# Four graph-attention layers on one core: the target scores of layers 0 and 2 go through DRAM instead of through TensorE

## The reference, cut to what matters

```python
# layer 0
f1 = (h @ W.T) @ a1;  f2 = (h @ W.T) @ a2            # a score per node: source, target
e = leaky_relu(f1[:, None] + f2[None, :], 0.2)
attn = softmax(where(adj == 0, -1e9, e), axis=-1)
x = x + elu(attn @ h)       # h >= 0 and attn >= 0, so elu changes nothing
# layer 2
e = leaky_relu((h @ w_src)[:, None] + (h @ w_dst)[None, :] + b, 0.2)
attn = softmax(where(adj + eye == 0, -inf, e), axis=-1)
x = x + attn @ h
```

## Time and profile before

| | |
|---|---|
| runs | 3770.13, 3774.3, 3774.59 us, median 3774.3 |
| profiled execution | 3771.3 us, of which the span of the trace is 3769.4 |
| TensorE busy | 3567.6 us, 95% of the span |
| VectorE busy | 3088.7 us, 82% |
| ScalarE, GpSimd busy | 52% and 50% |
| mean granted TensorE clock | 0.986 of full speed |

### The profile page before, as it was taken

The page is one execution under the profiler, slowest core; times in us unless marked ns, Lnnn a source line. Parts: engine busy times, 40 slices in busy tenths (PEclk is TensorE's granted clock), DMA queues, the critical chain, the costliest instruction groups (busy, mean ns, idle before and its releaser), DMA issues.

```text
span 3769.4 us, 75317 instructions
## 1 busy us (share of the span) xinstructions
PE 3567.6 (95%) x25488; PEld 3231.1 (86%) x25488; DVE 3088.7 (82%) x6892; ACT 1949.1 (52%) x4770; POOL 1867.9 (50%) x2852
## 2 busy tenths in 40 slices
PE   3899999999999999999999999999999999999996
PEld 2788888888888888888888888888888888888885
DVE  6788888888888888888888888888888888888874
ACT  2455555555555555555555555555555555555552
POOL 4355455445455545555554554554555545545543
PEclk7999999999999999999999999999999999999997
DMA  3000000000000000000000000000000000000000
GB/s 122 14 20 20 26 20 20 26 20 20 23 23 20 20 26 20 20 26 20 20 26 20 20 26 20 20 26 20 20 26 20 20 26 20 20 23 23 20 16 12
DMA packets 62512, 90.10 MB, mean 24 GB/s; under 512 B 9265, under 2 KB 25777, under 8 KB 62129
## 3 DMA queue, kind: packets, MB, share of 16 engines
q1 hardware_dynamic: 62128, 85.30, 6.9%
HBM read 51.72 MB, written 33.55 MB: 23 GB/s over the span
## 4 chain that ended last, share of the span: by engine, by line
PE 73%; DVE 16%; ACT 5%; issue 4%; POOL 1%; DVEq 0%; ACTq 0%; POOLq 0%
PE bank_c L360 20%; PE bank_b L360 18%; PE bank_e L360 10%; PE bank_e L401 6%; DVE product L805 5%; PE bank_a L368 4%; PE bank_e L380 4%; PE bank_e L335 3%; PE bank_b L335 3%; DVE g L1045 2%; DVE x L831 2%; DVE nlE L1016 2%; DVE nlE L1028 2%; ACT g_hi L740 2%; ACT xa L702 2%
## 5 line engine op out<-in xcount | busy, mean ns | idle before, releaser
L598 ACT ACTIVATE h<-x,rs 128x512 f32<-128x512 f32 x384 | 311.8, 812 | 383.5 <-POOL rs L1114 383.5
L360 PE MATMUL bank_c<-w_hi,g_hi 128*128 128x258 f32 x2048 | 433.2, 293 | 76.4 <-ACT g_hi L740 75.7
L1109 POOL TENSOR_SCALAR rs<-mv 128x1 f32<-128x1 f32 x512 | 142.0, 277 | 688.3 <-DVE mv L798 659.4
L1189 POOL TENSOR_TENSOR nlE<-nlE,nmE 128x512 f32<-128x512 f32 x256 | 265.9, 1038 | 416.1 <-DVE nmE L1036 416.1
L360 PE MATMUL bank_c<-w_lo,g_hi 128*128 128x258 f32 x2048 | 413.3, 283 | 0.0
L360 PE MATMUL bank_b<-w_lo,hT_hi 128*128 128x344 f32 x1536 | 409.3, 321 | 0.0
L360 PE MATMUL bank_b<-w_hi,hT_hi 128*128 128x344 f32 x1536 | 408.7, 320 | 0.0
L360 PEld LDWEIGHTS bank_c<-w_hi,g_hi 128*128 128x128 f32 x2048 | 314.8, 189 | 97.4 <-ACT g_hi L740 96.4
L360 PE MATMUL bank_c<-w_hi,g_lo 128*128 128x258 f32 x2048 | 350.7, 283 | 0.0
L360 PE MATMUL bank_b<-w_hi,hT_lo 128*128 128x344 f32 x1536 | 345.8, 320 | 0.0
L656 ACT ACTIVATE hT_hi<-bank_e 128x512 fp32r<-128x512 f32 x128 | 76.7, 600 | 499.6 <-PE bank_e L352 499.6
(11 more groups left out here) (158 smaller groups left out, 10294.7 us busy)
## 6 DMA issues: line engine op xcount, KB each, us to landing
x_in<-in_x SPq DMA_DIRECT2D x128, 256.0 KB, 2.6
out<-out_sb SPq DMA_DIRECT2D x128, 256.0 KB, 2.0
adj_in<-in_adj SPq DMA_DIRECT2D x128, 64.0 KB, 2.5
pTE<-in_L_gnn_att_src SPq DMA_DIRECT2D x1, 512.0 KB, 4.2
pE<-in_L_gnn_att_dst SPq DMA_DIRECT2D x1, 512.0 KB, 5.1
xl<-in_L_gnn_W SPq DMA_DIRECT2D x1, 512.0 KB, 6.0
x<-in_L_gnn_W SPq DMA_DIRECT2D x2, 256.0 KB, 5.7
out_sb<-in_L_gnn_W SPq DMA_DIRECT2D x2, 256.0 KB, 6.4
```

Source lines behind the costliest of these rows:

```text
L360: last = mm(bank[:, 0:width], a[:, c * P:(c + 1) * P], w[:, c, b * width:(b + 1) * width], start=(first and c == chunks[0] and n == 0), st ...
L598: activation(h[layer][:, 0, :], src, ACT.Relu, bias=rs[layer][:, 2:3], scale=rs[layer][:, 1:2])\
L1189: tt(nlE[:, half, :], nlE[:, half, :], nm, ALU.subtract).then_inc(sem(f"L3_shifted{i}"), 1)
```

## The change

TensorE no longer makes scores for layers 0 and 2: `scores_L0` and `scores_L2` are gone, and the waits that guarded `bank_a` move to the transposes of the exponentials. SP writes the target column to a small DRAM tensor, waits until it is there, and reads it back as a row in all 128 partitions (`t_all`), in a new step `spread_targets`. VectorE adds row, source column and mask in one instruction from SBUF. The target rows are negated once at the start, and the bias of layer 2 becomes the start value of the source column's sum. In SP's turn the new steps stand after the weight chunks: layer 2's, then the store, then layer 0's.

```diff
+        t_all = {i: sb(f"t_all{i}", [P, P]) for i in (0, 2)}
+        t_dram = {i: nc.dram_tensor(f"t_dram{i}", [2, P], F32, kind="Internal").ap() for i in (0, 2)}
...
+            def spread_targets(layer, g):
+                key, s = f"L{layer}", g.slot(2)
+                sp.wait_ge(sem(f"st_made{layer}"), g.made())
+                sp.wait_ge(sem(f"t_spread{layer}"), 16 * g.made(1))
+                sp.dma_start(t_dram[layer][s].rearrange("(n a) -> n a", a=1), st[layer][:, 1:2])\
+                    .then_inc(sem(f"t_sent{layer}"), 16)
+                sp.wait_ge(sem(f"t_sent{layer}"), 16 * g.made())
+                sp.wait_ge(sem(f"{key}_v"), g.made(1))
+                sp.dma_start(t_all[layer][:], t_dram[layer][s:s + 1, :].to_broadcast([P, P]))\
+                    .then_inc(sem(f"t_spread{layer}"), 16)
...
             def turn(t):
                 if t.graph(0).live:
                     load(t.graph(0))
-                if t.graph(6).live:
-                    store(t.graph(6))
                 if t.loop is None and t.step == 0:
                     load_rest()
                 if t.loop is None and t.step in (1, 2, 3):
                     stage_weights(prepared[t.step])
+                if t.graph(4).live:
+                    spread_targets(2, t.graph(4))
+                if t.graph(6).live:
+                    store(t.graph(6))
+                if t.graph(0).live:
+                    spread_targets(0, t.graph(0))
...
-                def scores_L0():
...
-                        masks_and_t(bank_a, m_l, m_r, [st[0][:, 1:2]]).then_inc(sem("L0_scores"), 1)
...
                 def turn_exp_L0():
                     if A.live:
                         pe.wait_ge(sem("L0_exp"), A.made())
+                        pe.wait_ge(sem("x1_made"), A.made(1))
+                        pe.wait_ge(sem("x3_made"), A.made(4))
...
-                def scores_L2():
...
-                        masks_and_t(bank_a, m_l, m_r, [st[2][:, 1:2]]).then_inc(sem("L2_scores"), 1)
...
                 def turn_exp_L2():
                     if Dg.live:
                         pe.wait_ge(sem("L2_exp"), Dg.made())
+                        if A.live:
+                            pe.wait_ge(sem("x1_made"), A.made())
+                        else:
+                            pe.wait_ge(sem("x3_made"), Dg.made(1))
...
+            first_of = {0: 0.0, 2: attn_b_all[:]}
+
-            def score_columns(layer, g, scores):
+            def score_columns(layer, g):
 
                 dve.wait_ge(sem(f"h_made{layer}"), g.made())
-                dve.wait_ge(sem(scores), g.made(1))
-                for i, row in enumerate((s_row, t_row)):
-                    last = nc.vector.tensor_tensor_reduce(product[:, layer + i, :], h[layer][:, 0, :], row[layer][:], 1.0, 0.0,
+                dve.wait_ge(sem(f"t_sent{layer}"), 16 * g.made(1))
+                dve.wait_ge(sem(f"L{layer}_v"), g.made(1))
+                for i, (row, first) in enumerate(((s_row, first_of[layer]), (t_row, 0.0))):
+                    last = nc.vector.tensor_tensor_reduce(product[:, layer + i, :], h[layer][:, 0, :], row[layer][:], 1.0, first,
                                                           ALU.mult, ALU.add, st[layer][:, i:i + 1])
...
+            def softmax_spread(layer, g, m):
+
+                key = f"L{layer}"
+                dve.wait_ge(sem(f"t_spread{layer}"), 16 * g.made())
+                dve.wait_ge(sem("masks_made"), g.made())
+                dve.wait_ge(sem(f"{key}_exp"), g.made(1))
+                stt(nl1[key][:], t_all[layer][:], st[layer][:, 0:1], m, ALU.add, ALU.add)\
+                    .then_inc(sem(f"{key}_v"), 1)
+                least(key, g)
...
-                        nc.vector.tensor_copy(t_row[0][:], bank_e[:, 1, :]).then_inc(sem("rows_made"), 1)
+                        ts(t_row[0][:], bank_e[:, 1, :], -1.0, None, ALU.mult).then_inc(sem("rows_made"), 1)
...
-                        ts(s_row[2][:], s_row[2][:], -1.0, None, ALU.mult).then_inc(sem("rows_made"), 1)
-                        dve.wait_ge(sem("rows_made"), 5)
+                        for row in (s_row[2], t_row[2], attn_b_all):
+                            ts(row[:], row[:], -1.0, None, ALU.mult).then_inc(sem("rows_made"), 1)
+                        dve.wait_ge(sem("rows_made"), 7)
...
-                        softmax_one("L0", A, bank_a[:, 0:P], st[0][:, 0:1])
+                        softmax_spread(0, A, mask[:, A.slot(MR), :])
...
-                        softmax_one("L2", Dg, bank_a[:, 0:P], st[2][:, 0:1], attn_b_all[:])
+                        softmax_spread(2, Dg, mask_loop[:, Dg.slot(MR), :])
```

More of the change, by code:

```diff
@@ L561, in turn @@
                 turn_h1()
-                scores_L0()
                 project_L1b_first()
@@ L569, in turn @@
                 scores_L1a()
-                scores_L2()
                 turn_h3()
@@ L798, in stats, with softmax_one, least @@
                 nc.vector.bn_aggr(mv[layer][:], bn[layer][:]).then_inc(sem(f"mv_made{layer}"), 1)
-            def score_columns(layer, g, scores):
+            first_of = {0: 0.0, 2: attn_b_all[:]}
+            def score_columns(layer, g):
                 dve.wait_ge(sem(f"h_made{layer}"), g.made())
-                dve.wait_ge(sem(scores), g.made(1))
-                for i, row in enumerate((s_row, t_row)):
-                    last = nc.vector.tensor_tensor_reduce(product[:, layer + i, :], h[layer][:, 0, :], row[layer][:], 1.0, 0.0,
+                dve.wait_ge(sem(f"t_sent{layer}"), 16 * g.made(1))
+                dve.wait_ge(sem(f"L{layer}_v"), g.made(1))
+                for i, (row, first) in enumerate(((s_row, first_of[layer]), (t_row, 0.0))):
+                    last = nc.vector.tensor_tensor_reduce(product[:, layer + i, :], h[layer][:, 0, :], row[layer][:], 1.0, first,
                                                           ALU.mult, ALU.add, st[layer][:, i:i + 1])
                 last.then_inc(sem(f"st_made{layer}"), 1)
-            def softmax_one(key, g, bank, ns, bias=None):
+            def softmax_one(key, g, bank, ns):
                 dve.wait_ge(sem(f"{key}_scores"), g.made())
                 dve.wait_ge(sem(f"{key}_exp"), g.made(1))
[L813 to L816, removed]
+                ts(nl1[key][:], bank, ns, None, ALU.add).then_inc(sem(f"{key}_v"), 1)
+                least(key, g)
[6 more added lines that the diff above has]
+                    .then_inc(sem(f"{key}_v"), 1)
+                least(key, g)
+            def least(key, g):
                 dve.wait_ge(sem(f"{key}_v"), g.made())
@@ L900, in columns_L2 @@
                     if Dg.live:
-                        score_columns(2, Dg, "L2_scores")
+                        score_columns(2, Dg)
                 def hT_lo_L1a():
@@ L920, in columns_L0 @@
                     if N0.live:
-                        score_columns(0, N0, "L0_scores")
+                        score_columns(0, N0)
                 def values_L1a():
```

## The result

| | before | after |
|---|---|---|
| runs on the same chip, median | 3773.91 us | 4642.37 us (4639.17 to 4645.38) |
| ratio, 95% interval | | 1.2304 [1.2282, 1.2325] |
| span of the profiled execution | 3769.4 us | 4637.3 us |
| mean granted TensorE clock | 0.986 | 0.915 |

The change makes the kernel 23% slower. I had forecast 3777 us with a range up to 3805: wrong by 865 us, in size and in kind.

What follows compares the result with a forecast made beforehand. TensorE sets the pace for 20.4 us of the 28.37 us turn, VectorE for 8.0. Turns give -0.06 us x 122 = -7.3 us, start-up +11.3, together +4.0; forecast 3777 us, range 3758 to 3805.

Steps and rivals of the forecast that it cites:

- the way over DRAM in the steady state: First-layer target column to DRAM and back as a row: 5.3 us against 7.2 us available, 1.9 us of cover.
- The rule named beside the sum: For the DRAM transfers: the skill's some 2.0 us fixed per transfer, so about 4 us for both.
- the row comes late: Rival: two transfers need over 7.2 us, stalling VectorE at the first-layer addition; 0.9 us x 122 = 110 us, 3885; chance 0.13.
- Start-up: Once, SP's new waits delay the `w2` chunk, turn 2's row and `w3` chunks: plus 11.3 us, bounds 6 and 13.
- Loads behind the row: SP's queue: next loads issued ten microseconds later, landing at about 2041, before their use after 2042.24; costs nothing.
- the hole: TensorE idle after the first layer's score matmuls, awaiting `g_hi`: widens from 0.62 to about 0.95 us, gain 0.00 us.
- The transposes of `turn_h3`: TensorE, third layer: start 0.15 us after VectorE's result, take 0.63 instead of 0.60 us; gain 0.13 us a turn.
- The first-layer addition: VectorE, both inputs now in SBUF: 0.35 instead of 0.34 us, plus 0.01 us a turn.
- the port rival: GpSimd's one-element step holds VectorE's first-layer addition: +0.08 to +0.29 us a turn, 3787 to 3812 us; chance 0.17.
- The start value: VectorE's products of `columns_L2`: per-partition `attn_b_all` instead of 0.0 costs 0.06 us a turn, bounds 0.00 and 0.06.
- The third-layer addition: VectorE: 0.05 us shorter but held beside GpSimd's output addition, ending at 2028.25 against 2028.26; worth nothing.
- The whole 0.33 us comes back: Rival: `out_read` doesn't bind TensorE at the third layer; 0.20 x 122 = 24 us more gain, 3753 us; chance 0.05.

Runs made afterwards that it cites:

- the fastest transfers: Changed kernel with the first layer's column written 512 bytes apart, the third's to SBUF, rows read from constants (other ends of the transfers): 3776.32 us.
- the line in both layers: Changed kernel with each column gathered into one SBUF partition's line, sent to DRAM in one 512-byte piece, then to all partitions: 3783.39 us, ratio 1.0026.
- the first experiment: Changed kernel with first- and third-layer additions taking the target row of the graph before, so none waits for a fresh row: 3826.43 us, ratio 1.0139.
- the run without a reader: Changed kernel with columns written at 8 bytes (first layer) and 4 bytes (third) from element to element, neither read back, rows constant: 3866.78 us.

## Why the prediction was wrong

**The step that failed** is the way over DRAM in the steady state, in the words of the prediction: "2.0 + 0.6 for the write, 0.1 to wake SP, 2.6 for the row: 5.3 us, and 1.9 us of cover". Measured: 7.1 for the write, less than 0.1 until the row is issued, 4.7 for the row: 11.9 us, 4.7 too late. The write was taken from transfers of 256 KB, in which each partition moves 2 KB; nothing in the trace before writes 4-byte elements side by side to DRAM. The 0.6 us that I had added for the small pieces came from the 0.89 us that SP spent on one issue; the write's issue takes 0.32 us, and what is slow comes behind it. The small load's 8.8 us would have been no better a guide. Its neighbours in the issues of the kernel before, the first issued just ahead of it and the second just behind:

```profile
t_row<-in_L_gnn_attn_w_dst SPq DMA_DIRECT2D x1, 256.0 KB, 9.0
...
b_att_all<-in_L_gnn_b_att SPq DMA_DIRECT2D x1, 4.0 KB, 9.3
```

They land as late at 500 and 8 times the size, so it was mostly the queue, as the prediction says. No row of the trace before could price this write; the fault was to take it for a large one's time with a small addition, and to give 0.13 to all that lies beyond the cover.

**The rule named beside the sum** differs as well. The Trainium skill (DMA: Bandwidth & Descriptors, Anatomy of one DMA) puts the fixed part at some 2 us, most of it the receipt from the target memory. It says so of transfers that GpSimd issues, and here SP issues them. In kind the trace fits. The windows of the kernel after, behind the write issued at 1998.88 (columns as above, DMA share next to last):

```profile
1999.50:2000.00 0.50, 0.50 (x6) 0.50 (x5) 0.50 (x2) 0.47 (x2) 0.00 (x0) 1.00 0.15 1
2000.00:2003.00 3.00, 2.06 (x10) 1.12 (x10) 2.97 (x6) 2.14 (x4) 1.04 (x1) 1.00 0.00 0
2003.00:2006.43 3.43, 3.43 (x28) 3.43 (x29) 2.97 (x6) 1.64 (x3) 2.10 (x3) 1.00 0.05 5
```

The DMA engines move something in the half microsecond and then nothing for 3 us, and SP still waits until 2006.4. (What moves in the last window, 5 GB/s for 3.43 us, is some 17 KB, and so not the 512 bytes of the column.) The trace doesn't say what SP's wait is for in that time. In size it doesn't agree: 1.4 us where the elements lie 16 bytes or more apart, 7.1 where they touch. The Trainium skill (DMA: Bandwidth & Descriptors, Specifications) also says that below 512 bytes the engines read, modify and write; that would touch all distances alike, and the runs show no cost of it at 16 bytes and more. What holds the touching elements was not found. Shown is only that it goes by their distance (1.4, 3.1, 7 to 8 us at 16, 8, 4 bytes), needs no reader, and goes away when the line is written in one piece. Why the row takes 4.7 instead of about 3 us is open as well; it does so only where it reads the very line that was just written with touching elements, since another line behind such a write (3.0) and a line just written in one piece (3.1) are both fast.

**The rival named for it**, "the row comes late", is what happened, but its price was 110 us, at 4.0 us for each transfer. Two terms were short: the lateness, 4.7 instead of 0.9 us (x 122: 570 us instead of 110), and the clock, which it didn't have (2.0 x 122: about 245 us).

**Start-up.** Predicted 11.3 us, bounds 6 and 13. Measured 54 in the kernel after, which includes the late rows of its first turns; 14.3 with the fastest transfers and 18.2 with the line in both layers. The mechanism was right in its three places, the `w2` chunk, the row of turn 2 and the `w3` chunk: VectorE waits 6.70, 4.10 and 2.01 us with the fastest transfers, and 8.55, 5.72 and 2.94 with the line, against my 6.0, 3.6 and 1.2. The row alone is 3.1 us, not 2.6. The sum also slips in itself: it takes the write at 2.0 us here, and the pair at 2.1 + 2.4, where the steady state has 2.6 + 0.1 + 2.6; with these it would have been 12.7 us instead of 11.3.

**Loads behind the row: "Nothing".** Wrong with slow writes (the first experiment's wait for `adj_in`), right with fast ones.

**What stood.** With the transfers inside their cover, five kernels with the start value have a period of 28.31 to 28.32 us (the one with other ends of the transfers 28.285), as predicted: 0.07 us below before, where I had -0.06. By parts: the hole is 0.94 us (predicted 0.95). The transposes of `turn_h3` start 0.14 us after `rE` ends and take 0.63 us, as at the earlier trace rows. The first-layer addition lasts 0.35 us, so the port rival is out: GpSimd's one-element step holds nobody. The start value costs 0.06 us. The third-layer addition takes 0.42 us where it overlaps GpSimd's output addition, and it costs nothing. "The whole 0.33 us comes back" is out as well. So the score matmuls were worth 0.13 us a turn, 16 us of 3771, before anything was paid for them, and all of it is the third layer's.

## What to carry to other kernels

A transfer is priced by the way its bytes lie and not by their number: before a column is made into a row through DRAM, measure that very access pattern alone, and prefer one long piece, even by an extra step (three transfers took 6.2 us here, two took 11.9). When a transfer gets onto the path, take its lateness times the turns, and if TensorE itself goes idle for microseconds, look at its clock behind the wait: here that added 2.0 us a turn to 4.7, and 0.7 to 2.0. And split a change that touches two places: the third layer's half is worth 0.25% with the fast transfers, while the first layer's half gives nothing and costs the start-up.

## What the runs showed of the hardware

- 128 elements of 4 bytes, one from each partition: 1.4 us to DRAM at distances of 16, 32, 64, 256 and 512 bytes, 3.1 at 8, 7.1 (6.3 to 9.4) at 4, and 7.8 at 4 in the run without a reader; 1.7 us into an SBUF column, 1.9 into one partition's line. One piece of 512 bytes from SBUF to DRAM: about 1.1 us from issue to issue.
- A line of 512 bytes from DRAM into all partitions: 2.8 to 3.2 us, where 128 different rows take 1.8 us; 4.7 us for a line that was just written with touching elements.
- TensorE idle for 0.94 us comes back at its full granted clock. Idle for 3.94 us and more its clock fell to 0.50 in each of 80 turns, for 2.0 us of lost work in the mean. Idle for 1.4 to 3.9 us it fell in 35 of 89 turns, and after 2.40 us it did both.
